# Scores from high and low parts, masks on ScalarE, and the new rows' gathers one window earlier

## Time and profile before

| what | value |
|---|---|
| median of 3 runs | 425.72 us |
| profiled execution, its own time | 422.87 us |
| its span, first to last instruction | 421.1 us |
| TensorE busy | 409.3 us (97%) |
| VectorE busy | 308.1 us (73%) |
| ScalarE busy | 240.8 us (57%) |
| GpSimd busy | 258.2 us (61%) |
| granted TensorE clock | 1.00 in the whole span |
| DMA | 65.15 MB, mean 155 GB/s |

### The profile page before, as it was taken

The page is one execution under the profiler, slowest core; times in us unless marked ns, Lnnn a source line. Parts: engine busy times, 40 slices in busy tenths (PEclk is TensorE's granted clock), DMA queues, the critical chain, the costliest instruction groups (busy, mean ns, idle before and its releaser), DMA issues.

```text
span 421.1 us, 9975 instructions
## 1 busy us (share of the span) xinstructions
PE 409.3 (97%) x2942; PEld 315.8 (75%) x2942; DVE 308.1 (73%) x901; ACT 240.8 (57%) x611; POOL 258.2 (61%) x230
## 2 busy tenths in 40 slices
PE   5999999999999988999999999999999999999997
PEld 1586877888945566888787878878778778888776
DVE  3798768769478586967978779687786787967742
ACT  4383433433267465756767567666676666765741
POOL 3206775275579877777777777777767777662000
PEclk9999999999999999999999999999999999999999
DMA  6616565157584455656555656565565655653321
GB/s 177 218 51 195 170 179 182 53 168 260 157 267 119 149 148 149 180 154 175 163 138 166 169 161 165 140 180 156 147 177 141 171 160 137 186 144 99 109 69 61
DMA packets 74107, 65.15 MB, mean 155 GB/s; under 512 B 50277, under 2 KB 52453, under 8 KB 74055
## 3 DMA queue, kind: packets, MB, share of 16 engines
q1 hardware_dynamic: 55088, 38.09, 31.3%
q0 software_dynamic: 15456, 22.08, 19.7%
q10 hardware_dynamic: 3510, 4.35, 2.9%
HBM read 74.46 MB, written 11.93 MB: 205 GB/s over the span
## 4 chain that ended last, share of the span: by engine, by line
PE 82%; DMA 5%; DVE 4%; POOL 4%; issue 4%; ACT 1%; SPq 0%; POOLq 0%; DVEq 0%; ACTq 0%
PE banks L1151 37%; PE banks L1141 11%; PE banks L1315 11%; PE banks L1294 9%; PE banks L1331 4%; PE banks L1167 3%; PE banks L1354 3%; PE banks L1344 2%; DMA wpt_late<-newkv,idx_all 1%; DMA newkv<-kvo 1%; POOL q_roots L497 1%; POOL wpt_late L524 1%; POOL windows L524 1%; DMA windows<-newkv,idx_all 1%; DMA xt_s<-xt_dram 1%
## 5 line engine op out<-in xcount | busy, mean ns | idle before, releaser
L524 POOL DMA_INDIRECT windows<-kvrows_dram,idx_all x78 | 83.0, 1064 | 31.1 <-issue 24.0
L524 POOL DMA_INDIRECT windows<-newkv,idx_all x78 | 81.8, 1049 | 29.0 <-issue 22.6
L655 ACT ACTIVATE pt_s<-banks 112x384 f32<-112x384 f32 x128 | 56.0, 496 | 61.9 <-PE banks L1141 56.9
L649 ACT ACTIVATE prob<-prob,negmax 128x336 f32<-128x336 f32 x128 | 72.4, 566 | 24.4 <-DVE negmax L1011 24.4
L1011 DVE CUSTOM_DVE_ANT_0 prob<-banks,mask 128x336 f32<-128x336 f32 x128 | 57.4, 503 | 2.7 <-PE banks L1294 1.2
L1021 DVE TENSOR_SCALAR prob<-prob,rinv 128x336 f32<-128x336 f32 x128 | 47.1, 410 | 2.3
L1294 PE MATMUL banks<-kt_s,qt_s 64*128 64x336 f32 x256 | 44.8, 468 | 0.0
L1315 PEld LDWEIGHTS banks<-pt_s,windows 112*64 112x64 f32 x624 | 33.3, 136 | 13.4 <-issue 10.9
L1315 PE MATMUL banks<-pt_s,windows 112*64 112x128 f32 x624 | 42.7, 279 | 0.0
L1151 PE MATMUL banks<-wf_hi,x 128*128 128x512 f32 x120 | 41.1, 403 | 0.0
L1141 PE MATMUL banks<-ident_r,prob_w 128*112 128x128 f32 x384 | 40.4, 242 | 0.0
(11 more groups left out here) (222 smaller groups left out, 918.2 us busy)
## 6 DMA issues: line engine op xcount, KB each, us to landing
usel<-utab SPq DMA_DIRECT2D x64, 128.0 KB
xt_s<-xt_dram SPq DMA_DIRECT2D x16, 256.0 KB, 3.7
newkv<-kvo SPq DMA_DIRECT2D x16, 256.0 KB, 2.6
stage<-xtok_dram SPq DMA_DIRECT2D x16, 256.0 KB, 11.3
tsel<-ttab SPq DMA_DIRECT2D x64, 64.0 KB
out_dram<-xo ACTq DMA_DIRECT2D x15, 256.0 KB
windows<-kvrows_dram,idx_all POOLq DMA_INDIRECT x78
windows<-newkv,idx_all POOLq DMA_INDIRECT x78
```

Source lines behind the costliest of these rows:

```text
L524: P.indirect_dma_start(kv_s[i][:, c, :], None, newkv if new else kvrows, bass.IndirectOffsetOnAxis(ap=idx_all[:, new * CH + c, b:b + 1], a ...
L649: A.activation(pr, pr, ACT.Exp, bias=negmax[:, g:g + 1], scale=-1.0, accum_out=psum_p[b % 2][:, g:g + 1]).then_inc(S["exp_done"], 1)
L655: A.activation(pt_s[g][:], tb[g % 2][0:KP, 0:CH * 128].rearrange("p (c q) -> p c q", c=CH), ACT.Copy).then_inc(S["pt_ev"], 1)
```

## The change

- **Gathers** (GpSimd): the new rows of batch `k+3` instead of `k+2` are gathered in iteration `k`, and the old rows of batch 4 after the new rows of batch 3.
- **Scores**: keys and queries are split into a high part (ScalarE's copy to `float32r`) and a low part (VectorE's `low`); `scores` has twelve `float32r` products in place of four float32 ones. The high and low parts take the place of two buffers that were used in turn, so that there is now one pair.
- **Masks** are copied by ScalarE (`mask_at` between the second and the third `probs_ev`).
- **Queries**: the two sine products move from `query_first` (even iterations) to `query_sines`, in odd iterations.
- **Values** are one function; `mix(t-1)` stands ahead of it.
- **SyncE** reads one register a tile (`picks`), worked out beforehand by VectorE, and takes the indices from it by division and remainder.
- `combined(3)` stands ahead of `scores(0)`; new semaphores and buffer names (`qt_f`) go with the above.

```diff
@@ sync, load_tile
+                both = sp.value_load(picks[0:1, t:t + 1], min_val=0, max_val=PICKS * PICKS - 1)
+                pick = [both % PICKS, both // PICKS]
                 for u in range(2):
-                    s = sp.value_load(subj_s[0:1, 2 * t + u:2 * t + u + 1], min_val=0, max_val=7)
+                    s = pick[u] % 8
...
-                    a2 = sp.value_load(ad2_s[0:1, 2 * t + u:2 * t + u + 1], min_val=0, max_val=NE2 - 1)
-                    a3 = sp.value_load(ad3_s[0:1, 2 * t + u:2 * t + u + 1], min_val=0, max_val=NE3 - 1)
-                    a23 = sp.value_load(pair_s[0:1, 2 * t + u:2 * t + u + 1], min_val=0, max_val=NE2 * NE3 - 1)
+                    a23 = pick[u] // 8
+                    a2, a3 = a23 % NE2, a23 // NE2
@@ gpsimd, main loop
             for k in range(NB):
-                if k == 0:
-                    pool.wait_ge(S["comb_ev"], NE3 // 2)
-                    gather(4, 0)
-                    continue
-                if k + 2 < NB:
-                    gather(k + 2, 1)
+                if k + 3 < NB:
+                    gather(k + 3, 1)
                 if k + 4 < NB:
-                    pool.wait_ge(S["pv_mm"], k)
+                    if k == 0:
+                        pool.wait_ge(S["comb_ev"], NE3 // 2)
+                    else:
+                        pool.wait_ge(S["pv_mm"], k)
                     gather(k + 4, 0)
@@ scalar
-                    after(act, S["s_mm"], 4 * (b - 2) + 2 * p + 2)
-                    A.activation(kt_s[b % 2][p][:], sbk[p][:, 0:WK], ACT.Copy).then_inc(S["kt_ev"], 1)
+                    after(act, S["s_mm"], 4 * (b - 1) + 2 * p + 2)
+                    A.activation(kt_s[0][p][:], sbk[p][:, 0:WK], ACT.Copy).then_inc(S["kt_ev"], 1)
...
+            def mask_at(b):
+                after(act, S["negs_ready"], 4 * (b - 1))
+                o = act.value_load(offi[0:1, b:b + 1], min_val=0, max_val=SHIFT)
+                A.activation(mask[b % 2][:], masktab[:, bass.ds(o, WK)], ACT.Copy).then_inc(S["mask_ready"], 1)
...
                     probs_ev(k, 0)
                     probs_ev(k, 1)
+                    mask_at(n)
@@ vector
+            def query_sines(t):
...
+                V.tensor_tensor(t2[:, :, 0:32], src[:, :, 32:64], sin[:, :, 0:32].to_broadcast([128, 8, 32]), ALU.mult)
+                V.tensor_tensor(t2[:, :, 32:64], src[:, :, 0:32], sin[:, :, 32:64].to_broadcast([128, 8, 32]), ALU.mult).then_inc(S["q_sin"], 1)
...
+            def query_low(t):
+                low(qt_s[0][:], qt_s[1][:], sbk[2][:], "qt_ev", t + 1, "qt_lo")
+
+            def keys_low(b):
+                for p in range(2):
+                    low(kt_s[0][p][:], kt_s[1][p][:], sbk[p][:, 0:WK], "kt_ev", 2 * b + p + 1, "kt_lo")
...
                 if k % 2 == 0:
-                    mask_at(n)
+                    keys_low(n)
...
                     if n < NB:
-                        mask_at(n)
+                        query_low(t + 1)
+                        keys_low(n)
+                    if t + 2 < TILES:
+                        query_sines(t + 2)
                     if t >= 1:
                         ranks(t - 1)
@@ tensor
             def scores(b):
-                pe.wait_ge(S["qt_ev"], t + 1)
-                pe.wait_ge(S["kt_ev"], 2 * b + 2)
+                pe.wait_ge(S["qt_lo"], t + 1)
+                pe.wait_ge(S["kt_lo"], 2 * b + 2)
                 after(pe, S["negs_ready"], 4 * b)
-                for g in range(G):
-                    p, h = g // 2, g % 2
-                    if g == 3 and u == 0:
+                for p in range(2):
+                    if p == 1 and u == 0:
                         after(pe, S["z_hi"], t - 1)
-                    r = slice(64 * h, 64 * h + 64)
                     cols = slice(256 * p + 128 * u, 256 * p + 128 * u + 128)
-                    mm(sbk[g][:, 0:WK], qt_s[t % 2][r, cols], kt_s[b % 2][p][r, :], start=True, stop=True).then_inc(S["s_mm"], 1)
+                    for i, j in ((0, 0), (0, 1), (1, 0)):
+                        for h in range(2):
+                            r = slice(64 * h, 64 * h + 64)
+                            last = mm(sbk[2 * p + h][:, 0:WK], qt_s[i][r, cols], kt_s[j][p][r, :], start=(i == j), stop=(i == 1))
+                            if i == 1:
+                                last.then_inc(S["s_mm"], 1)
...
             scores(0)
-            combined(3)
...
                     scores(n)
-                    values(k, 0)
                     if t >= 1:
                         mix(t - 1)
-                    values(k, 1)
+                    values(k)
```

More of the change, by code:

```diff
@@ L149, in build @@
         adf = sb("adf", [1, 3, NB])
-        pair_s = sb("pair_s", [1, NB], i32)
+        picks = sb("picks", [1, TILES], i32)
+        PICKS = 8 * NE2 * NE3
         pos = sb("pos", [128, TILES])
@@ L174, in build @@
         qrot = sb("qrot", [128, 512])
-        qt_s = [sb(f"qt_s{i}", [128, 512]) for i in range(2)]
+        qt_s = words([(f"qt_{w}", [128, 512]) for w in ("hi", "lo")])
+        qt_f = [sb(f"qt_f{i}", [128, 512])[:] for i in range(2)]
         negmax = sb("negmax", [128, G])
@@ L223, in build @@
         prob = [sb(f"prob{i}", [128, G, WK]) for i in range(3)]
-        kt_s = [[sb(f"kt_s{i}{p}", [128, WK]) for p in range(2)] for i in range(2)]
+        kt_s = [[sb(f"kt_{w}{p}", [128, WK], f32r) for p in range(2)] for w in ("hi", "lo")]
         pt_s = [sb(f"pt_s{i}", [KP, CH, 128]) for i in range(G)]
@@ L667, in queries_ev @@
                 act.wait_ge(S["qt_mm"], t + 1)
-                after(act, S["s_mm"], 8 * (t - 1))
-                A.activation(qt_s[t % 2][:], sbk[2][:], ACT.Copy).then_inc(S["qt_ev"], 1)
+                after(act, S["s_mm"], 8 * t)
+                A.activation(qt_s[0][:], sbk[2][:], ACT.Copy).then_inc(S["qt_ev"], 1)
             def mixed_high(t):
@@ L697, in _ @@
             evac(u2p[1][0], u2c[1], "comb_ev", "u2_hi", 2)
+            act.wait_ge(S["meta_ready"], 1)
+            act.wait_ge(S["l_mask"], 16)
+            mask_at(0)
             for g in range(G):
@@ L731, in _ @@
                     probs_ev(k, 1)
+                    if n < NB:
+                        mask_at(n)
                     if t == 0:
@@ L893, in index_rows @@
                     w = bank[6 + i][0:BLOCK, 0:HR]
-                    has = (qrot, qt_s[0])[i][0:BLOCK, 0:HR]
+                    has = (qrot[:], qt_f[0])[i][0:BLOCK, 0:HR]
                     V.tensor_scalar(none[:, h], w, 0.0, float(NONE), ALU.is_equal, ALU.mult)
@@ L907, in meta @@
                 V.tensor_copy(adf[:, 0, :], ad2_s[:])
-                link(V.tensor_copy(adf[:, 1, :], ad3_s[:]))
-                link(V.scalar_tensor_tensor(adf[:, 2, :], adf[:, 1, :], float(NE2), adf[:, 0, :], ALU.mult, ALU.add))
-                V.tensor_copy(pair_s[:], adf[:, 2, :]).then_inc(S["meta_ready"], 1)
+                V.tensor_copy(adf[:, 1, :], ad3_s[:])
+                link(V.tensor_copy(adf[:, 2, :], subj_s[:]))
+                link(V.scalar_tensor_tensor(adf[:, 0, :], adf[:, 1, :], float(NE2), adf[:, 0, :], ALU.mult, ALU.add))
+                link(V.scalar_tensor_tensor(adf[:, 2, :], adf[:, 0, :], 8.0, adf[:, 2, :], ALU.mult, ALU.add))
+                two = adf[:, 2, :].rearrange("a (t u) -> a t u", u=2)
+                V.scalar_tensor_tensor(picks[:], two[:, :, 1], float(PICKS), two[:, :, 0], ALU.mult, ALU.add).then_inc(S["meta_ready"], 1)
                 dve.wait_ge(S["l_w1tab"], 16)
@@ L927, in query_first @@
                     dve.wait_ge(S["qtab_ready"], 1)
+                after(dve, S["q_n"], t)
+                src = qraw[:, t, :].rearrange("p (h d) -> p h d", h=8)
+                sin = sintab["q"][:, t:t + 1, :]
+                V.tensor_tensor(t2[:, :, 0:32], src[:, :, 32:64], sin[:, :, 0:32].to_broadcast([128, 8, 32]), ALU.mult)
+                V.tensor_tensor(t2[:, :, 32:64], src[:, :, 0:32], sin[:, :, 32:64].to_broadcast([128, 8, 32]), ALU.mult).then_inc(S["q_sin"], 1)
+            def query_first(t):
                 after(dve, S["q_rot"], t)
                 src = qraw[:, t, :].rearrange("p (h d) -> p h d", h=8)
[L930 to L934 removed]
+                V.tensor_tensor(t1[:], src, costab["q"][:, t:t + 1, :].to_broadcast([128, 8, 64]), ALU.mult).then_inc(S["q_cos"], 1)
+                dve.wait_ge(S["q_cos"], t + 1)
+                dve.wait_ge(S["q_sin"], t + 1)
                 V.tensor_tensor(t1[:], t1[:], t2[:], ALU.add).then_inc(S["q_n"], 1)
@@ L1090, in _ @@
                 if k % 2 == 0:
-                    mask_at(n)
+                    keys_low(n)
+                    if t == 0:
+                        query_sines(1)
                     if t + 1 < TILES:
@@ L1309, in values @@
                     pe.wait_ge(S["wf_ev"], 1)
-                pe.wait_ge(S["pt_ev"], 4 * b + 2 * p + 2)
-                for c in range(CH):
-                    for h in range(2):
-                        g = 2 * p + h
-                        col = 256 * u + 128 * p
```

(13 more changed lines are left out.)

31 lines of the change are left out of this document (11 added, 20 removed).

## The result

The changed kernel takes 536.69 us (median of 4 runs, 535.29 to 538.79), the kernel before 425.95 us (4 runs, 424.01 to 426.9). The ratio is 1.261, 95% interval 1.255 to 1.267: slower by about 111 us. The forecast was 505 us with a range of 455 to 555.

What follows compares the result with a forecast made beforehand. TensorE bound the kernel before at 8.65 us an iteration; GpSimd was to bind after. `keys_t(4)` at 158.80, 27 periods of 11.63 us, 27.7 less 0.3 after, plus 1.77 and 2.85, gave 505 us, range 455 to 555.

Steps and rivals of the forecast that it cites:

- The mechanism: GpSimd's gathers: new rows directly follow the same batch's old rows, so GpSimd waits for a landing each iteration; period 11.63 us.
- Waits for `kt_lo` or in front of `mix`: TensorE waits in front of `scores` or `mix`: named as signs that the prediction was wrong.
- the other signs: GpSimd's wait some 100 us, TensorE's at `keys_t` some 85 us, TensorE busy about 80%, a tile about 23 us.
- L: GpSimd: time from the start of a batch's last old gather to its first new one, taken as 4.88 us.
- The 3.37: Landing of new rows read where `keys_t` waited, 3.37 us, taken as the nearest row for a quiet landing.
- The 7.12: Last old to first new gather of batch 31 at the loop's end, 7.12 us, taken as a landing in traffic.
- The sum: Whole kernel: `keys_t(4)` at 158.80, 27 periods of 11.63 us, the end stretch and run offsets give 505 us.
- All landings in traffic: Rival at GpSimd's gathers: each landing costs 7.12 us, 570 us in all; chance 0.15.
- All quiet: Rival at GpSimd's gathers: every landing takes 3.37 us, 461 us in all; chance 0.15.
- The other side: Rival at GpSimd's wait for old rows: the landing hides, TensorE stays the bound, 414 us; chance 0.07.
- The clock: Rival on TensorE: stops each iteration lower its clock to 1.2 GHz throughout, over 640 us; chance 0.03.
- The terms costed at nothing: Low parts, masks, sines, `mix`, picks, buffers and start: each taken as 0 us, hidden by TensorE's work or GpSimd's wait.

Runs made afterwards that it cites:

- e2: The kernel before with the new order of gathers alone: 531.74 us, ratio 1.248.
- e11: The changed kernel with the old order of gathers and each `usel` load split by rows into two loads: 419.40 us, ratio 0.983.
- e19: The changed kernel, new order of gathers, with `usel` and `tsel` loaded for the first two tiles only: 484.40 us, one run.
- e13: The changed kernel, new order of gathers, with each `usel` load split by rows into two loads: 497.58 us, ratio 1.163.
- e1: The changed kernel with the old order of gathers, all other edits kept: 434.47 us, ratio 1.0175.
- e6: The changed kernel with the old order of gathers and SyncE's register loads as before in place of packed `picks`: 427.97 us, ratio 1.0018.

## Why the prediction came out as it did

**The mechanism was right.** The order of the gathers puts a landing between old and new rows of one batch in each iteration, and e2 shows it alone to be the loss. Waits for `kt_lo` or in front of `mix` did not appear. Of the other signs, GpSimd's wait came out at 150 us where 100 was forecast (L = 4.88 would have been 28 × 3.89 = 109) and a tile at 26.3 us where 23 was. TensorE's waits (88.7 us, forecast 85) and its busy share (81%, forecast 80%) were hit by luck: the period was longer than forecast, but TensorE was busy for 260.0 of the 348.1 us of the 27 iterations, where 27 of e11's take 229, at a mean granted clock of 0.84 (1.00 in e11).

**The size of L was not.** The step that failed: "of a tile's two landings I expect one in traffic and one in quiet ... L = 4.88". Measured, L is 5.36 of idle and 0.99 of the gather before it, 6.35 us on average; only 8 of 28 landings had less than 4 us of idle, and 20 had 4.45 to 7.15. Three things were wrong in it.

- The 3.37 is not the quiet end of old rows: the shortest of the 28 is 3.00 + 0.99 = 3.99, and in e19, with most of SyncE's loads gone, the mean is still 4.56.
- The 3.37 was not a quiet landing either. The microsecond of the earlier trace rows with a DMA share of 0.14 (145 to 146) lies before that gather starts at 146.12. Over the whole of the three landings the share is 0.50 (3.37 us), 0.56 (5.66) and 0.49 (7.12), and tells no short one from a long one.
- The 7.12 of the earlier trace rows was not a row "with this very order", since three new gathers lay in between; no row before had it. It was still the only timing of old rows among the rows, and nearer to the mean than 4.88; it got a quarter of the weight.

The mean DMA share is the wrong sign here. These are two landings of the changed kernel, from the last old gather to the first new one; columns as in the earlier trace rows.

```profile
289.94:297.98 8.04, 4.54 (x19) 3.92 (x20) 1.59 (x4) 2.09 (x5) 0.99 (x1) 0.50 0.25 80
...
304.44:308.91 4.47, 4.43 (x31) 3.68 (x29) 3.91 (x10) 3.23 (x10) 1.11 (x1) 1.00 0.64 167
```

The long one has the lower share (0.25 against 0.64), and VectorE is hardly busy in it (1.59 of 8.04 us), so VectorE doesn't hold it up. The same holds over all: ten of the twelve landings with 6 us of idle or more have a share of 0.22 to 0.39, seven of the eight with less than 4 us one of 0.49 to 0.66. In e13, with `usel` split, it turns round: twelve of the 13 landings with more than 4 us of idle have 0.72 to 0.88, twelve of the 15 shorter ones 0.24 to 0.36. That fits loads of `usel` that hold a few of the 16 DMA engines while the others stand idle; which engines they were, no row shows. The period came out at 13.02 where 11.63 was forecast.

**The sum, term by term.** `keys_t(4)` starts at 161.18 (forecast 158.80, + 2.4: the gathers came 1.3 later, the first old rows landed 0.8 sooner than 4.88, the new rows 2.0 later). 27 iterations to `keys_t(31)` at 509.29 take 348.1 (314.0, + 34.1). Then 27.7 to the end (27.4). That is 36.8 us on the span. The median lies 2.1 below the profiled execution, where 2.85 above was assumed, and this gives back 5: 505 + 36.8 − 5 = 536.8, measured 536.7.

**The rivals.** "All landings in traffic", 570, has the right direction and an L 0.8 too long. "All quiet" and the Trainium skill's fit of 2.0 us plus bytes ("DMA: Bandwidth & Descriptors", Anatomy of one DMA — SWDGE (gpsimd) path; an estimate of 2.5 us by it) lie below every one of the 28 landings. The other side, 414 us, was wrong twice: the landing doesn't hide, and where it does (e1) the kernel gives 434, since the `usel` loads are the next bound. I had looked for what becomes late only among the engines, not among the queues.

**The clock.** It fell, but not as the rival had it. TensorE's timeline of the changed kernel, after its longest stop:

```profile
268.02 0.99 PE L1170 MATMUL banks<-ident_r,windows_w 112*128 112x112 f32 x6 [8.01 <-DMA windows<-newkv,idx_all]
...
271.33 0.63 PE L1180 MATMUL banks<-wf_lo,x 128*128 128x512 f32 x1
...
273.19 0.39 PE L1180 MATMUL banks<-wf_lo,x 128*128 128x512 f32 x1
```

After 8.01 us without work a product takes 0.63 us, and from 272.5 on 0.39. The stretches above say the same: granted 0.50 (the 1.2 GHz level) from 263 to 272, 1.00 from 274. It costs the loop nothing that the rows show, since GpSimd sets the period and never waited for TensorE in the loop.

**The terms costed at nothing** were hidden as said, but only under GpSimd's wait. In the loop that TensorE bounds, the scores save 0.13 to 0.21 us an iteration (1.12 and 1.20 in e11 against 1.33), not 0.27: the pairs do run together, most of them 0.15 us apart, but the first takes 0.25 until the next begins, and in e11's odd iterations so does the fourth. Scores (0.34 a tile) and `mix` with `values` (2.55 against 2.70 before, 0.15) would make a tile 0.49 shorter; it is 0.32 shorter. Most of the rest is a wait of TensorE for VectorE: in e11 the products with `wo` begin 1.95 us after `up` (235.05 to 237.00), in the kernel before 1.82 (254.09 to 255.91), both 0.06 us after VectorE has ended `ot_lo`. `mix` is a gain of 0.15 a tile, the masks' move one of 0.41 against leaving them on VectorE beside the new low parts, and `picks` a loss of some 6.5 us in 15 tiles as long as the loads of `usel` crowd.

## What to carry to other kernels

When an in-order engine issues a gather and then something that must wait for that gather's landing, put other issues in between: with the same six gathers an iteration, TensorE sets 8.65 us in one order, and GpSimd 13 in the other. Price such a landing with a row of the same kind of transfer, even if there is only one, rather than with a mean over kinder ones, and look what its row has in between. Don't read the traffic from the DMA share of one microsecond, nor from the mean share alone: here the slowest landings fell where that was low. When an edit frees the bound, look at the load queues too: an edit that only lets a queue issue faster can lose (e1 against e6), and a load whose outermost dimension is 2 can be the next bound (e1 against e11).

## What the runs showed of the hardware that was not expected

- After a stop of TensorE of 3.18 us (e1) or 8.01 us (changed kernel) the clock is granted at 0.50 for a while (225.5 to 228.5, and until 272), and dense products take 0.63 in place of 0.39 us. The single idle microsecond of the earlier trace rows had shown nothing of it.
- SyncE's issue of one load can itself take long: up to 6.47 us for one of `usel` in e1, up to 1.69 in e11, where the same bytes are split by rows.
- The shortest landing of old rows took 3.6 us from the last issue's start (2.62 + 0.99 in e19), with `usel` and `tsel` gone from the loop.
- Long landings can go with a low mean DMA share: 0.25 in one of 8.04 us, 0.64 in one of 4.47.
